# A gated cross-attention block on one core: softmax sums on two rows a head, and another order at both ends

## The reference

```
x1  = x  + tanh(g_xattn) * attention(layernorm(x), context)      # 16 heads of 32, causal
out = x1 + tanh(g_ffn)   * ffn(layernorm(x1))                    # 512 -> 1408 (gate, up) -> 512
attention: q = n @ Wq.T ; k, v = split(context @ Wkv.T) ; softmax(q k^T / sqrt(32), causal) @ v @ Wout.T
ffn:       rows of x and of the weights are rounded to fp8 (e4m3) with a scale of 448 / max|row|;
           t = silu(g) * u ; t is rounded in the same way ; y = t @ w_down.T
```

## Time and profile before

| what | value |
|---|---|
| median of 3 runs | 727.99 us (727.42 to 729.45) |
| the profiled execution's own time | 729.19 us |
| span of the profiled execution | 727.4 us |
| mean granted TensorE clock | 0.978 of full speed |
| busy: PE, DVE, ACT, POOL | 657.9, 680.1, 555.5, 538.5 us |
| HBM traffic | 31.59 MB read, 9.83 MB written |

### The profile page before, as it was taken

How to read it: one execution, slowest core, us unless ns; L and a number is a source line. 1 busy time by engine, 2 the same in 40 slices (tenths; PEclk the granted TensorE clock), 3 DMA queues, 4 the chain that set the end, 5 groups by cost and what they waited for, 6 DMA issues and landing times.

```text
span 727.4 us, 15637 instructions
## 1 busy us (share of the span) xinstructions
PE 657.9 (90%) x6091; PEld 419.9 (58%) x6160; DVE 680.1 (93%) x1127; ACT 555.5 (76%) x995; POOL 538.5 (74%) x601
## 2 busy tenths in 40 slices
PE   1758698999999999999999999999999999998794
PEld 1647476666566666566565657566566556545342
DVE  4999998989899999999999999999999999999997
ACT  6896878987869787878878787979797867555642
POOL 6768889796968778687878686968696677666651
PEclk9888999999999999999999999999999999999997
DMA  8887768385795757585867566675775686512121
GB/s 303 223 153 199 157 147 176 80 176 94 123 158 107 152 105 154 80 181 96 167 108 141 111 144 116 132 144 114 155 123 116 90 150 100 111 22 87 27 70 58
DMA packets 143479, 93.57 MB, mean 129 GB/s; under 512 B 107598, under 2 KB 114126, under 8 KB 143406
## 3 DMA queue, kind: packets, MB, share of 16 engines
q1 hardware_dynamic: 141246, 90.74, 61.6%
q0 software_dynamic: 576, 1.45, 0.8%
q10 hardware_dynamic: 1584, 0.39, 0.3%
HBM read 31.59 MB, written 9.83 MB: 57 GB/s over the span
## 4 chain that ended last, share of the span: by engine, by line
PE 47%; DVE 29%; POOL 11%; DMA 5%; issue 3%; ACT 3%; SPq 0%; ACTq 0%; DVEq 0%
PE pair L1153 26%; DVE mx L3116 5%; POOL PT L793 4%; PE pair L1411 4%; PE pair L1416 3%; DVE room L2943 2%; DVE room L2947 2%; PE pair L1394 2%; DVE room L3260 2%; PE pair L1440 2%; DVE room L3308 2%; PE pair L1436 2%; POOL room L832 2%; DVE tm L3323 2%; DVE wmax L2962 2%
## 5 line engine op out<-in xcount | busy, mean ns | idle before, releaser
L832 POOL TENSOR_TENSOR room<-room,up_scale 128x512 f32<-128x512 f32 (+1 forms) x96 | 125.6, 1312 | 63.1 <-ACT room L2349 62.2
L3116 DVE TENSOR_REDUCE mx<-pair 128x6 f32<-128x768 f32 x128 | 117.6, 947 | 1.7 <-PE pair L1343 1.4
L793 POOL TENSOR_SCALAR_AFFINE_SELECT PT<-PT 128x512 f32<-128x512 f32 x128 | 104.0, 841 | 13.1 <-ACT PT L2274 13.0
L2274 ACT ACTIVATE PT<-pair 128x768 f32<-128x768 f32 x128 | 98.3, 814 | 9.4 <-PE pair L1394 7.8
L1153 PE MATMUL pair<-WgT,room 128*128 128x512 bf16 (+1 forms) x382 | 89.5, 366 | 2.5 <-DVE room L3447 0.8
L1153 PE MATMUL pair<-xT,WqTh 128*128 128x256 bf16 x512 | 86.5, 272 | 1.5 <-ACT WdT L2037 1.3
L1153 PE MATMUL pair<-WuT,room 128*128 128x512 bf16 (+1 forms) x368 | 84.8, 361 | 3.3 <-DVE room L3260 1.4
L2349 ACT ACTIVATE room<-room,sx 128x512 f32<-128x512 f32 (+1 forms) x96 | 65.2, 682 | 24.2 <-DVE room L3260 18.8
L1153 PE MATMUL pair<-WdT,room 128*128 128x512 bf16 x326 | 75.4, 379 | 3.1 <-DMA room<-room 2.9
L2381 ACT ACTIVATE room<-room 128x512 bf16<-128x512 f32 (+1 forms) x96 | 55.8, 586 | 21.2 <-DVE room L3308 21.1
L1153 PE MATMUL pair<-xT,WqTl 128*128 128x256 bf16 x256 | 69.7, 272 | 0.0
(11 more groups left out here) (151 smaller groups left out, 1863.4 us busy)
## 6 DMA issues: line engine op xcount, KB each, us to landing
xin<-in_x_dram SPq DMA_DIRECT2D x16, 512.0 KB, 4.0
x<-in_x_dram SPq DMA_DIRECT2D x16, 512.0 KB, 4.8
K<-kh SPq DMA_DIRECT2D x32, 256.0 KB, 4.9
Q<-qh SPq DMA_DIRECT2D x32, 256.0 KB, 4.6
out_dram<-x SPq DMA_DIRECT2D x15, 512.0 KB, 3.0
K<-kl SPq DMA_DIRECT2D x16, 256.0 KB, 6.1
Q<-kl SPq DMA_DIRECT2D x16, 256.0 KB, 4.2
room<-in_L_ffn_w_down_dram SPq DMA_DIRECT2D x4, 704.0 KB, 9.0
```

Of the source, the lines that this page charges most:

```text
L793: pool.affine_select(out=view, in_=view, compare_op=ALU.is_ge, fill=0.0, base=0, pattern=[[0, 2], [0, 2], [1, P]], channel_multiplier=-1). ...
L832: pool.tensor_tensor(g, g, up_scale[:, chunk(n)[1]], ALU.mult).then_inc(slw_done, 1)
L2274: act.activation(head_columns(ring(b, c), 0, 384), head_columns(shifted_pair[c][:, :], 0, 384), ACT.Exp, scale=SCALE).then_inc(exp_done, 1)
L3116: dve.tensor_reduce(mx[:, heads, :], head_columns(w, 0, 3 * P).rearrange("p h (r s) -> p h r s", s=P), AX.X, ALU.max).then_inc(max_done, 1)
```

## The change

Four things change.

The sums use two rows a head. Row g holds the sums of queries 0 to 127, row 4 + g those of queries 128 to 255, and the bank is 128 columns wide. A head now takes three products of 128 columns (keys 0 to 127 for each half of the queries, keys 128 to 255 for the second half), all of which accumulate in the same 128 columns; the weights, `pick[:, g, :]` or `pick[:, 4 + g, :]` (ones in every eighth column), decide the row. The reciprocal is 128 x 128, and there are eight shuffles of 128 columns.

```
-        pick = sb("pick", [P, KT, HD])
+        pick_flat = sb("pick_flat", [P, TT * KT * (HD + 1)])
+        pick = pick_flat[:, 0:TT * KT * HD].rearrange("p (v c) -> p v c", c=HD)
+        pick_ones = pick_flat[:, :].rearrange("p (v c) -> p v c", c=HD + 1)
-        rsum = sb("rsum", [P, S])
+        rsum = sb("rsum", [P, P])
...
-                for t in range(TT):
-                    for j in range(G):
-                        last = pe.matmul(sum_bank[HD * j:HD * j + HD, t * P:S], pick[:, g, :],
-                                         probabilities(b, 2 * g + j // 2, j % 2, t), start=(g == 0 and t == 0),
-                                         stop=(g == KT - 1 and t == TT - 1), skip_group_check=True)
+                for j in range(G):
+                    pe.matmul(sum_bank[HD * j:HD * j + HD, 0:P], pick[:, g, :], probabilities(b, 2 * g + j // 2, j % 2, 0)[:, 0:P],
+                              start=(g == 0), stop=False, skip_group_check=True)
+                for j in range(G):
+                    pe.matmul(sum_bank[HD * j:HD * j + HD, 0:P], pick[:, KT + g, :], probabilities(b, 2 * g + j // 2, j % 2, 0)[:, P:S],
+                              start=False, stop=False, skip_group_check=True)
+                for j in range(G):
+                    last = pe.matmul(sum_bank[HD * j:HD * j + HD, 0:P], pick[:, KT + g, :], probabilities(b, 2 * g + j // 2, j % 2, 1),
+                                     start=False, stop=(g == KT - 1), skip_group_check=True)
...
-                dve.reciprocal(rsum[:, :], sum_bank[:, 0:S]).then_inc(rsum_done, 1)
+                dve.reciprocal(rsum[:, :], sum_bank[:, 0:P]).then_inc(rsum_done, 1)
...
-                dve.stream_shuffle(out=R[:, 2 * h, :], in_=rsum[:, :], mask=[2 * h] * HD)
-                dve.stream_shuffle(out=R[:, 2 * h + 1, :], in_=rsum[:, :], mask=[2 * h + 1] * HD).then_inc(r_spread, 1)
+                for g in range(2 * h, 2 * h + 2):
+                    for t in range(TT):
+                        last = dve.stream_shuffle(out=R[:, g, tok(t)], in_=rsum[:, :], mask=[KT * t + g] * HD)
+                last.then_inc(r_spread, 1)
```

```
             load_w_kv()
+            load_x(0)
+            unit_loaded(0)
             load_c(0)
-            unit_loaded(0)
-            load_x(0)
             unit_loaded(1)
...
             load_w_q()
-            load_x1(0)
-            load_c(1)
             turn_x(0, 0)
```

The beginning and the end of the lists of all five queues are put in another order; the lines of the loop stay. An extract from VectorE's list (beginning) and from POOL's:

```
             unit_maxima(0)
+            put_keys(1)
             put_queries(0)
-            put_keys(0)
             unit_maxima(1)
             pair_inverse(0)
+            unit_maxima(2)
             pair_scales(0)
+            unit_maxima(3)
             unit_floored(1)
-            unit_maxima(3)
+            pair_inverse(1)
             unit_floored(0)
-            unit_maxima(2)
-            pair_inverse(1)
...
+            keys_low(3, 0)
             c_low(4)
-            keys_low(3, 0)
-            down_placed(9)
+            keys_low(3, 1)
+            down_placed(1)
+            down_placed(10)
+            down_placed(2)
+            down_placed(3)
+            max_parts(2)
             up_scaled(0, 0)
-            max_parts(2)
             up_scaled(0, 1)
```

More of the change, by code:

```diff
@@ L847, in _ @@
             constant(pool.memset(minus_half[:, :], -0.5))
-            constant(pool.memset(pick[:, :, :], 0.0))
-            for g in range(KT):
-                constant(pool.memset(pick[:, g, :].rearrange("p (a b) -> p a b", b=4)[:, :, g:g + 1], 1.0))
+            constant(pool.memset(pick_flat[:, :], 0.0))
+            for a in range(HD // (TT * KT)):
+                constant(pool.memset(pick_ones[:, :, TT * KT * a:TT * KT * a + 1], 1.0))
             assert n_const == N_CONST_PE
@@ L884, in _ @@
             queries_low(0, 0)
+            queries_low(0, 1)
             x_low(1, 1)
-            queries_low(0, 1)
+            attention_weights_low(7)
             unit_rounded(5)
+            unit_rounded(7)
             keys_low(1, 0)
-            unit_rounded(7)
-            down_placed(2)
-            attention_weights_low(8)
+            keys_low(1, 1)
             c_low(2)
-            down_placed(0)
-            keys_low(1, 1)
             max_parts(0)
@@ L897, in _ @@
             unit_rounded(9)
+            x_low(2, 0)
+            queries_low(1, 0)
+            queries_low(1, 1)
             causal_part(0, 0)
@@ L958, in _ @@
             causal_part(2, 2)
-            queries_low(3, 0)
             causal_part(2, 3)
-            up_scaled(0, 4)
+            queries_low(3, 1)
             causal_part(2, 4)
@@ L965, in _ @@
             causal_part(2, 7)
+            rstd2_made(1)
+            x_low(4, 0)
             up_scaled(0, 5)
-            queries_low(3, 1)
-            x_low(4, 0)
-            rstd2_made(1)
             x_low(4, 1)
@@ L975, in _ @@
             up_scaled(1, 0)
+            keys_low(4, 1)
             up_scaled(1, 1)
@@ L978, in _ @@
             up_scaled(1, 2)
+            scales1(5)
             up_scaled(1, 3)
-            keys_low(4, 1)
+            queries_low(4, 0)
+            queries_low(4, 1)
             up_scaled(1, 4)
-            scales1(5)
-            up_scaled(1, 5)
             causal_part(3, 0)
@@ L1029, in _ @@
             normalised_low(11, 1)
+            added(9, 0)
             up_scaled(10, 0)
-            added(9, 0)
             keys_low(13, 0)
+            keys_low(13, 1)
+            max_parts(12)
             up_scaled(10, 1)
-            max_parts(12)
-            keys_low(13, 1)
             up_scaled(10, 2)
             up_scaled(10, 3)
+            c_low(14)
+            up_scaled(10, 4)
             queries_low(13, 0)
-            up_scaled(10, 4)
-            c_low(14)
+            scales1(14)
             queries_low(13, 1)
@@ L3504, in _ @@
             maxima(0, 6)
+            maxima(0, 7)
+            unit_maxima(8)
+            second_maxima(0)
             pair_inverse(4)
-            maxima(0, 7)
             pair_scales(4)
-            second_maxima(0)
             unit_floored(9)
@@ L3860, in _ @@
             rounded_x(13, 1)
+            maxima(15, 0)
             sums_inverted(14)
```

2185 lines of the change are left out of this document (1149 added, 1036 removed).

## The result

The changed kernel takes 735.09 us (median of 7 runs, 733.03 to 738.07), the kernel before 728.02 us in the same comparison (7 runs, 727.30 to 729.60). The ratio is 1.0094, with a 95% interval from 1.0076 to 1.0112: it is slower by 7 us. The forecast was 724.9 us with a range that ended at 730.8, so it was wrong, in its sign too. The profiled execution of after took 737.95 us around a span of 736.2; it is one of the two longest of the seven, so the two profiles lie 8.8 us apart (729.19 before) where the medians lie 7.1.

What follows compares the result with a forecast made beforehand. The prediction took TensorE to bound the loop and VectorE both ends. Its terms, 0 - 1.8 + 0.2 - 1.2 - 0.3 = -3.1 us against the median of 727.99, gave 724.9 us, range 720.0 to 730.8.

Steps and rivals of the forecast that it cites:

- The sums, the reciprocal, the shuffles: Per-piece times of the two-row form: 0.66 us a group of sums, 950 ns a reciprocal, 0.212 us a shuffle.
- The slow feed: Rival, 5%: TensorE's short matmuls are fed too slowly, 40 ns a pair, costing 15.6 us: 743.6 us.
- The rows: Two-row sums with narrower reciprocal and shuffles: -0.48 us a batch where it counts, -1.8 us in all.
- The place: Where the two-row saving counts: -1.4 us in batches 13 to 15, -0.4 in batches 0 and 1, 0 in the loop.
- The first transfers: x instead of the context ahead of unit 0: 1.3 us later, 1.1 hidden by the wait for constants, +0.2 us.
- The order of the beginning: Reordered steps up to 140 us: a fifth of VectorE's 6.4 us of idle time comes back, -1.2 us.
- The blocked queue: Rival, slower, 17%: four down_placed in a row on GpSimd delay max_parts(2) in the beginning, +3.9 us: 730.4 us.
- The order of the end: Reordered steps from 620 to 728 us, taken as swaps of neighbours: -0.3 us, ends -2.5 and +2.
- The loop: Batches 2 to 12, bound by TensorE: VectorE's saving counts 0 and the start-to-start time stays as it was.

Runs made afterwards that it cites:

- plain before: The kernel before with its 92 DMA transposes replaced by plain copies of the same bytes: 727.94 us, ratio 0.9993 to the kernel before.
- begin only: plain before with the beginning of all five lists, first transfers included, in the order of after; end and sums as before: 734.16 us, 1.0075.
- cuts_between: begin only with GpSimd's c_low(3) and eight cuts put back between the low parts, as in before: 733.70 us, 1.0067.
- before_cuts_in_a_row: plain before with GpSimd's eight cuts of batch 1 in one row behind the scatter and low parts: 733.07 us, 1.0053.
- end_up_later: plain before with after's order of the end, but largest_x_inverted(11) and rounded_t(10, 0) put back ahead of up(10, 3) and up(10, 4): 729.30 us, 1.0003.
- scatter_later: The kernel after with plain copies, GpSimd's down_placed(0) moved behind queries_low(2, 0), queries_low(2, 1) and c_low(3): 736.30 us, 1.0105.

## Why the prediction was wrong

*The sums, the reciprocal, the shuffles: right.* 0.65 us a group against 0.66, 956 ns against 950, 0.207 us against 0.212. The slow feed (5%) is refuted by the first. The rows were put at -1.8 us and measured -2.1. The place was half right: the end gave 1.5 more (from 1.4 us ahead at batch 11 to 2.9 at batch 15), as forecast with 1.4; the beginning gave 0.4 at batch 1, as allowed, but 1.4 to 1.6 in batches 4 to 8. These are differences of two single profiles.

*The first transfers: right.* Unit 0 at 9.74 us, no wait for the constants, and putting the old order back gains nothing.

*The order of the beginning: wrong, +5.5 us where I took -1.2.* The step that failed is the term "a fifth, -1.2 us, as the net of steps pulled ahead of their users". It rests on: "The set of VectorE instructions ahead of `second_maxima(0)` is the same in both lists. So that point can move only by idle time, not by work." The premise is not quite true: `pair_inverse(4)` and `pair_scales(4)` now stand behind that point, about half a microsecond. The conclusion came true (68.54 us started, inside what I allowed), and it says nothing of the next stretch or of new idle time. Ahead of `second_maxima(1)` the sets differ: `unit_maxima(12)` and `unit_maxima(13)` now stand behind it, 1.80 us at 104.49, and the scales of two pairs of units have changed places. Up to 104 us VectorE has done 14 unit maxima instead of 16. Busy time up to 104 us and up to the reciprocal of batch 1, first before, then after:

```profile
0.00:104.00 104.00, 66.50 (x623) 53.43 (x629) 91.97 (x135) 83.33 (x140) 80.82 (x99) 0.90 0.79 200
...
0.00:121.63 121.63, 82.37 (x826) 63.55 (x834) 107.34 (x155) 96.40 (x163) 97.23 (x114) 0.92 0.79 194
```

```profile
0.00:104.00 104.00, 68.66 (x655) 53.65 (x656) 87.84 (x137) 81.38 (x138) 78.17 (x94) 0.87 0.81 201
...
0.00:127.56 127.56, 88.01 (x901) 66.50 (x902) 107.22 (x163) 95.98 (x162) 94.70 (x114) 0.87 0.77 180
```

`second_maxima(1)` is on time (102.5 and 102.4 us) and looks like proof that nothing is lost, but VectorE's busy time is 4.1 us less, with 3.9 more idle in the first 60 us (new are 2.42 for unit 7, 1.08 for TensorE, 0.56 for ScalarE, and a first unit 1.37 later; waits of 1.09 for the constants and 0.39 for a unit are gone). Not all of the 4.1 us is work put off. The same step can take longer in one kernel: `second_maxima(0)` took 1.53 us before and 0.17 after. The reciprocal and shuffles are cheaper too. The pair of equal form, plain before and begin only, differs by 2.2 us of busy time at 104 us (90.93 and 88.72), which is little more than the two maxima.

The lower lines show what the beginning lost. Up to the reciprocal of batch 1 VectorE is busy for the same time, 107.34 and 107.22 us; the whole delay is idle time, 14.3 us before and 20.3 after. 3.9 us of the 6.0 arise in the first 60 us. In the last stretch VectorE waits 3.08 us for TensorE at 126.09, which had itself waited 3.95 us for `residual(0, 1)`, the step behind the held instruction. So in after the hold costs VectorE no more than the many smaller stretchings of before did; it costs because of what stands behind it. In `cuts_between`, with a hold of 9.24 us, it does cost work: 111.45 us busy up to that reciprocal.

All nine profiles with the new beginning show 14 maxima at 104 us, 14.0 to 14.6 us of idle time in the first 60, and a late reciprocal of batch 1, between 124.7 and 127.6 us, whichever single step was put back. I read the early idle time and the maxima put off as the reason why removing one wait only showed the next. That is argued, not shown. Against it stands `before_cuts_in_a_row`: 16 maxima at 104 us, 10.7 us of idle time in the first 60, and the reciprocal at 126.7 all the same, by late cuts alone. So a late reciprocal does not prove the debt. A kernel with the two maxima back in front and `unit_loaded(7)` ahead of `stack_keys(0, 2)` was not tried, and how the 5.5 us divide between the early idle time and the chain of waits at 110 to 127 us stays open. Part of the shift of the milestone is no loss: in after `maxima(2, 0)` (0.95 us) stands ahead of this reciprocal, before it stood behind.

*The blocked queue (17%): the right sign and the wrong mechanism.* The total, 735.09, is beyond even its 730.4. Its own test, `max_parts(2)` not after 139 us, failed (143.74), but `second_maxima(2)` was itself at 142.83. Moving the step ahead of the scatters cost 9 us.

*The order of the end: wrong, +2.6 us where I took -0.3.* I wrote that "The moves there are swaps of neighbours". One of these swaps, `up(10, 3)` and `up(10, 4)` ahead of `largest_x_inverted(11)` and `rounded_t(10, 0)`, is the whole loss by the totals: `up(10, 3)` overwrites the rows that `added(9, 1)` still reads, and I never asked what the first instruction of a swapped pair waits for. `end_up_later` shows that.

*The loop: right.* The period is unchanged, and it carried the lost time on.

The prediction had named the sign that its reasons are wrong: the beginning, up to `turned_maxima(2)`, moves by more than 3 us. It moved by 5 (from 139.7 to 144.9 us).

Of the kernels measured, the two-row sums with before's order of both ends are the fastest: 726.29 us against 728.53 for before in the same group, and in the form with plain copies.

## What to carry to other kernels

When a list is reordered, compare busy time, idle time and the steps done by the bounding engine up to each milestone, not the milestone alone: one that is on time may have been paid for with work pushed behind it. Count the steps too, since busy time also grows when two engines slow each other. Before calling a swap of neighbours free, look up what the step that moves forward waits for, and what now stands behind that wait. And where one wait is removed and another of the same size appears, that wait was not the loss by itself; look further ahead in the same stretch.

## What the runs showed of the hardware

In all nine profiles with the new beginning one VectorE instruction was held: for 5.51 to 5.52 us in four of them (a bf16 `tensor_scalar` of 512 columns, which takes 0.34 us where nothing slows it), for 4.58, 4.60, 4.60 and 4.36 us in the next four, for 9.24 us in `cuts_between`. GpSimd ran without a pause for all or nearly all of that time (in `scatter_later` it paused for 0.24 us). In before the same kinds of work overlap for 12 us (110 to 122) with both engines slowed: no VectorE instruction over 2.17 us, and five cuts in a row at 1.17 us each instead of 0.6:

```profile
114.13 5.87 POOL L793 TENSOR_SCALAR_AFFINE_SELECT PT<-PT 128x512 f32<-128x512 f32 x5
```

"SBUF — State Buffer" in the Trainium skill, section "SBUF: two separate sides", says that the pair of ports that VectorE and GpSimd share is locked by one of them for a whole instruction. The hold of 5.52 us lasts while seven GpSimd instructions end one after another, which goes beyond that; the measurement decides. What picks between taking turns and a hold is open. In the nine, GpSimd's unbroken run begins with a scatter, in the six others it begins after a wait; but before has a run from 143.42 us that begins with a scatter and holds nothing for over 2.11 us, and a beginning without scatters in that stretch was not tried.

TensorE's granted clock is also lower in the beginning of after: 0.91 in 60 to 140 us, against 0.95 and 1.00. Up to the reciprocal of batch 1 it is 0.87 against 0.92 in the lines above. In the pair of equal form TensorE is busy for 85.64 us up to that point in begin only (837 matmul records, clock 0.89) and for 82.35 in plain before (826 records, 0.92). So some of the late reciprocal may be a slower TensorE; what that costs by itself was not taken apart.
